# A weight-composing token kernel on one core: the first batch of the token stage gets an order of its own on VectorE and ScalarE, the two parts of B3 are made ahead of the last weight pass, and one low part of W1 is made a step sooner

## What is computed

```python
x = x + L0(x)   # x @ W0.T + (x @ A0[label0]) @ B0.T * 0.5
x = x + L1(x)   # x @ w_eff.T,  w_eff = quantised(W1 + delta) * scale + delta,  delta = B1 @ A1 * 0.5
x = x + L2(x)   # x @ W2.T + (x @ A2[label2]) @ B2.T * 0.5
x = x + L3(x)   # x @ W3.T + 2 * sum_e gate[e] * (x @ A3[e].T) @ B3[e].T
# gate: softmax over the best two of the 8 logits x @ Wr.T (+5 on the label's expert)
```

## Time and profile before

| | |
|---|---|
| median of 3 runs | 611.8 us (611.38 to 611.91) |
| the profiled execution | 611.85 us, its span 609.9 us |
| TensorE busy | 599.9 us, 98% of the span |
| VectorE / ScalarE / GpSimd busy | 392.5 (64%) / 214.0 (35%) / 80.4 us (13%) |
| granted clock of TensorE | full in all 40 slices |
| chain that ended last | PE 85%, DVE 10%, ACT 2%, DMA 2%, issue 1% |

### The profile page before, as it was taken

How to read it: one execution, slowest core, us unless ns; L and a number is a source line. 1 busy time by engine, 2 the same in 40 slices (tenths; PEclk the granted TensorE clock), 3 DMA queues, 4 the chain that set the end, 5 groups by cost and what they waited for, 6 DMA issues and landing times.

```text
span 609.9 us, 9220 instructions
## 1 busy us (share of the span) xinstructions
PE 599.9 (98%) x3247; PEld 536.0 (88%) x3247; DVE 392.5 (64%) x726; ACT 214.0 (35%) x402; POOL 80.4 (13%) x111
## 2 busy tenths in 40 slices
PE   7999999999999999999999999899999999999998
PEld 7999999899999999888888687688888888888887
DVE  3589998999998829100005688957474747475653
ACT  4444133346233138211111378433333333333331
POOL 2101010023000000000000015040404040403120
PEclk9999999999999999999999999999999999999999
DMA  9963220361000030200001200121221213130201
GB/s 266 261 170 99 82 70 1 43 218 68 1 1 1 1 35 7 38 1 0 0 0 34 69 2 2 52 87 54 85 75 63 82 56 98 39 118 19 96 8 70
DMA packets 57823, 37.68 MB, mean 62 GB/s; under 512 B 26684, under 2 KB 51516, under 8 KB 57796
## 3 DMA queue, kind: packets, MB, share of 16 engines
q1 hardware_dynamic: 57796, 37.31, 21.8%
HBM read 28.91 MB, written 8.39 MB: 61 GB/s over the span
## 4 chain that ended last, share of the span: by engine, by line
PE 85%; DVE 10%; ACT 2%; DMA 2%; issue 1%; SPq 0%; POOL 0%; DVEq 0%
PE acc L1356 46%; PE acc L1493 27%; PE acc L1514 4%; DVE q L1010 2%; PE acc L1516 2%; PE aux L1343 2%; DVE hg_lo L1036 1%; PE acc L1522 1%; DVE qtmp L1009 1%; PE acc L1523 1%; PE aux L1431 1%; DMA a_t<-in_L_cond_Wr_dram 1%; PE acc L1343 1%; DVE w_lo L914 1%; DMA w_raw<-in_L_cond_lora_B_w_dram 1%
## 5 line engine op out<-in xcount | busy, mean ns | idle before, releaser
L1356 PE MATMUL acc<-hg_hi,w_hi 128*128 128x352 f32 (+2 forms) x384 | 87.2, 335 | 0.4 <-DVE hg_lo L921 0.4
L1356 PE MATMUL acc<-hg_lo,w_hi 128*128 128x352 f32 (+2 forms) x384 | 85.8, 331 | 0.0
L1356 PE MATMUL acc<-hg_hi,w_lo 128*128 128x352 f32 (+2 forms) x384 | 85.7, 331 | 0.0
L1356 PEld LDWEIGHTS acc<-hg_hi,w_hi 128*128 128x128 f32 x384 | 66.3, 188 | 1.7 <-DVE hg_lo L921 0.6
L1356 PEld LDWEIGHTS acc<-hg_hi,w_lo 128*128 128x128 f32 x384 | 67.3, 188 | 0.0
L1356 PEld LDWEIGHTS acc<-hg_lo,w_hi 128*128 128x128 f32 x384 | 67.3, 188 | 0.0
L914 DVE TENSOR_TENSOR w_lo<-a_t,w_hi 128x1024 fp32r<-128x1024 f32 (+2 forms) x9 | 9.9, 1106 | 82.1 <-ACT w_hi L596 82.1
L1010 DVE TENSOR_TENSOR q<-q,qtmp 128x1024 f32<-128x1024 f32 x48 | 60.0, 1250 | 1.7
L761 ACT CAST left_hi<-xr 128x512 fp32r<-128x512 f32 x64 | 39.7, 622 | 54.4 <-PE acc L1493 34.7
L1493 PE MATMUL acc<-rh_a,left_hi 128*128 128x512 f32 (+1 forms) x132 | 52.7, 399 | 0.0
L532 POOL TENSOR_TENSOR xr<-xr 128x512 f32<-128x512 f32 x28 | 35.5, 1287 | 130.5 <-DVE left_lo L1159 129.2
(11 more groups left out here) (213 smaller groups left out, 1041.8 us busy)
## 6 DMA issues: line engine op xcount, KB each, us to landing
x_st<-in_x_dram SPq DMA_DIRECT2D x64, 128.0 KB, 2.8
out_dram<-part SPq DMA_DIRECT2D x31, 256.0 KB, 2.8
g<-in_L_cond_W_dram SPq DMA_DIRECT2D x8, 512.0 KB, 7.3
w_st<-in_L_cond_W_dram SPq DMA_DIRECT2D x8, 512.0 KB, 4.7
a_t<-in_L_cond_weight_dram SPq DMA_DIRECT2D x8, 512.0 KB, 5.0
w_raw<-in_L_cond_weight_dram SPq DMA_DIRECT2D x8, 512.0 KB, 4.0
a_raw<-in_L_cond_lora_A_dram SPq DMA_DIRECT2D x5, 128.0 KB, 3.6
a_raw<-in_L_cond_lora_A_dram SPq DMA_DIRECT2D x20, 32.0 KB, 2.0
```

What stands on the lines that cost most here:

```text
L1356: last = pe.matmul(acc[0:a.shape[-1], slot, bank * BANK:bank * BANK + c1 - c0], a[:, k, :], b[:, k, c0:c1], start=(at == 0 and n == 0), st ...
```

## The change

It has three parts.

1. In the second weight stage VectorE makes `w1_low(3)` ahead of `quantise(5, 2)` instead of behind it.
2. B3's high part (now two tiles of 512 columns at other places, `b3_hi0` and `b3_hi1`) and its low part are made just ahead of the last weight pass, where they were made in batch 0. The small tiles `hg`, `gate`, `top_i` and `hl1` change places with them.
3. Batch 0 of the token stage has its own written order on ScalarE and VectorE. The sum `S3` is split after `S2` and `S1` (tuple `LEFT_FIRST`, function `left_count`), and TensorE gets a wait for `S3` ahead of `M7`. The order of TensorE's products, GpSimd's list and SyncE's list stay as they are, and so does every other batch on ScalarE and VectorE.

```diff
+    LEFT_FIRST = ("A12", "A11", "A21", "A22", "S2", "S1", "S3", "S4")
...
-        b3_hi = place("b3_hi", 32768, [P, D], F32R)
+        b3_hi = [place("b3_hi0", 203776, [P, HD], F32R), place("b3_hi1", 126720, [P, HD], F32R)]
...
             evacuate(bp[0:R, :], 0, R, R, C_ALL)
+            act.wait_ge(b3_copied, 1)
+            for half in range(2):
+                act.copy(b3_hi[half][:], b3_f[:, half * HD:(half + 1) * HD]).then_inc(b3_hd, 1)
...
             add_delta(6)
+            w1_low(3)
             quantise(5, 2)
-            w1_low(3)
...
             add_bp(slice(0, R), 0, slice(0, R), C_ALL)
+            for half in range(2):
+                dve.wait_ge(b3_hd, half + 1)
+                cols = slice(half * HD, (half + 1) * HD)
+                dve.tensor_tensor(b3_lo[:, cols], b3_f[:, cols], b3_hi[half][:].bitcast(F32),
+                                  ALU.subtract).then_inc(b3_done, 1)
...
                 if first:
-                    pe.wait_ge(b3_done, 1)
+                    pe.wait_ge(b3_done, 2)
                 finish("Y", 0, 0)
 
+                wait_left("S3")
                 pe.wait_ge(part_copied, count(b, COPIES, "M6"))
```

VectorE's new list of batch 0 (ScalarE's follows the same pattern):

```diff
+                if first:
+
+                    v_copy(0)
+                    right_low("B21", 3)
+                    v_low(0)
+                    v_copy(1)
+                    right_low("T4", 3)
+                    m_low(0)
+                    v_low(1)
+                    left_low(b, "S2")
+                    right_low("T2", 3)
+                    best_two(0)
+                    m_low(1)
+                    gated(0)
+                    left_low(b, "S1")
+                    right_low("T1", 3)
+                    best_two(1)
+                    gated(1)
+                    g_low(0)
+                    left_low(b, "S3")
+                    for k in range(HALF):
+                        third_low(k)
+                    left_low(b, "S4")
+                    right_low("B22", 0)
+                    g_low(1)
+                    dve.wait_ge(l_split, LEFT.index("S4") + 1)
+                    x_turn(b, 0, 1)
+                    for k in range(1, HALF):
+                        right_low("B22", k)
+                    out("C11", "Y", "F11", "M1")
+                    left_low(b, "A12", 1)
+                    left_low(b, "A11", 1)
+                    out("C21", "W", "F21", "M7")
+                    out("C22", "X", "F22", "M5")
+                    sel_low(b + (E_FIRST + 1))
+                    x_turn(b, 1, 1)
+                    left_low(b, "A21", 1)
+                    left_low(b, "A22", 1)
+                    out("C12", "Z", "F12", "M6")
+                    return
```

More of the change, by code:

```diff
@@ L97, in count, with left_count @@
         return b * len(names) + (ahead * len(names) + names.index(name) + 1)
+    def left_count(b, name, ahead=0):
+        if isinstance(b, int) and b == 0 and not ahead:
+            return LEFT_FIRST.index(name) + 1
+        return count(b, LEFT, name, ahead)
     RIGHT = (("B11", 0), ("B21", 0), ("T4", 0), ("B11", 1), ("B21", 1), ("T4", 1), ("B11", 2), ("B21", 2), ("T4", 2),
@@ L857, in exponential @@
                     act.activation(gate[:, 24:25], gate[:, 25:26], ACT.Exp).then_inc(e_ready, 1)
-                if not first:
-                    copy_part("M1", "X")
+                if first:
+                    copy_second(0)
+                    right_high("T4", 3)
+                    v_high(0)
+                    copy_second(1)
+                    left_high(b, "S2")
+                    m_high(0)
+                    v_high(1)
+                    right_high("T2", 3)
+                    copy_part("M1", "X")
+                    done("M2")
+                    left_high(b, "S1")
+                    m_high(1)
+                    right_high("T1", 3)
+                    exponential(0)
+                    left_high(b, "S3")
+                    for k in range(HALF):
+                        third_high(k)
+                    done("M4")
+                    left_high(b, "S4")
+                    exponential(1)
+                    g_high(0)
+                    copy_part("M6", "X")
+                    for k in range(HALF):
+                        right_high("B22", k)
+                    act.wait_ge(sel_ready, SEL_FIRST + 2)
+                    sel_high()
+                    copy_part("M5", "Z")
+                    g_high(1)
+                    copy_part("M7", "X")
+                    left_high(b, "A12", 1)
+                    left_high(b, "A11", 1)
+                    left_high(b, "A21", 1)
+                    done("M3")
+                    left_high(b, "A22", 1)
+                    return
+                copy_part("M1", "X")
                 copy_second(0)
                 left_high(b, "S3")
-                if first:
-                    right_high("T4", 3)
                 v_high(0)
-                if first:
-                    right_high("T2", 3)
                 copy_second(1)
@@ L1157, in left_low @@
             def left_low(b, name, ahead=0):
-                dve.wait_ge(l_hd, count(b, LEFT, name, ahead))
+                dve.wait_ge(l_hd, left_count(b, name, ahead))
                 dve.tensor_tensor(left_lo[:, SLOT[name]], RAW[name], left_hi[:, SLOT[name]].bitcast(F32),
@@ L1320, in pair @@
                     left_low(b, "A21", 1)
[L1321 to L1325, removed]
-                out("C22", "X", "F22", "M5")
[L1327 to L1334, removed]
+                    out("C22", "X", "F22", "M5")
+                    left_low(b, "A22", 1)
+                    out("C12", "Z", "F12", "M6")
+                    return
+                dve.wait_ge(part_copied, count(b, COPIES, "M5"))
+                c12 = parts[PART_OF["C12"]][:]
+                add_or_take(c12, c12, parts[PART_OF["M5"]][:], ALU.add, last_sum)
+                out("C22", "X", "F22", "M5")
+                dve.wait_ge(last_sum, 1)
+                out("C12", "Y", "M3", "M6", HALVES[0])
+                out("C12", "W", "F12", "M6", HALVES[1])
             base = link.n
@@ L1523, in finish @@
                     pe.matmul(at, vm[h][:], vb_lo[:, cols], start=False, stop=False, skip_group_check=True)
-                    three(at, (hgt_h[h][:], hgt_l[h][:]), (b3_hi[:, cols], b3_lo[:, cols]),
+                    three(at, (hgt_h[h][:], hgt_l[h][:]), (b3_hi[half][:, c], b3_lo[:, cols]),
                           stop=True).then_inc(step_done, 1)
```

50 lines of the change are left out of this document (13 added, 37 removed).

## The result

The changed kernel took 608.05 us, the median of 5 runs (607.4 to 609.49); the kernel before took 611.86 on the same chip, also 5 runs (611.38 to 612.13). The ratio is 0.9941, 95% interval 0.9926 to 0.9955: 3.8 us faster, against a forecast of 608.3. The profiled execution took 607.86 us.

What follows compares the result with a forecast made beforehand. TensorE, busy 98% of the span, was taken as the bound, so only its pauses could yield gain. Batch 0 -3.9, batch 1's head +0.2, part 1 +0.25: -3.45 from 611.8 gives 608.3 us, range 607.3 to 609.4.

Steps and rivals of the forecast that it cites:

- Part 1: Second weight stage: the pause at delta(7) goes, but VectorE idles 1.6 us and pass 14 starts later; +0.25 us, a loss.
- Part 2: Ahead of the last weight pass: 1.9 us of VectorE's idle time cover 1.2 us of work; cost 0.
- Part 3: Batch 0 of the token stage: of 4.61 us lost, 0.4 stays at turn_v(0) and 0.3 at W; -3.9 us.
- a sign of being wrong: Batch 0: VectorE's second gate, forecast to end at 383.1, ending after 383.5 would show the prediction wrong.
- Head of batch 1: Start of batch 1: GpSimd's later sums hold VectorE's low part of S3; +0.2 us, bounds 0 and +1.3.
- Rival 1: Second weight stage: pass 14 isn't held by VectorE, 0.5 us gained instead of 0.25 lost; 607.6 us, chance 0.08.
- Rival 2: Batch 0: VectorE becomes the bound, an early 0.5 us delay is paid once, plus batch 1's hold; 609.95 us, chance 0.14.
- Rival 3: Batch 1: the hold takes all four GpSimd sums, 2.8 us lost instead of 0.2; 610.95 us, chance 0.04.
- Rival 4: After batch 0: VectorE's lag costs 0.6 us at mix(0) in each of 7 batches; 612.35 us, chance 0.03.

Runs made afterwards that it cites:

- B3 alone: Kernel before with only the two parts of B3 made ahead of the last weight pass, batch 0 in its old order: 610.14 us, ratio 0.9983.
- the tail alone: Kernel before with the new order only behind batch 0's second gate, on ScalarE and VectorE; B3 as before: 609.65 us, ratio 0.9973.
- B3 late: Changed kernel with B3's parts made in batch 0 again, just ahead of g_low(0): 608.86 us, ratio 0.996 to the kernel before.
- part 1 alone: Kernel before with only w1_low(3) moved ahead of quantise(5, 2): 611.81 us, ratio 1.0003.
- the third experiment: Kernel before with, in batch 0, g_high(1) ahead of ScalarE's cast of A12 and g_low(1) ahead of VectorE's transposes: 613.53 us, ratio 1.0028.
- more sums on GpSimd: Changed kernel with two spare 128 x 512 operations on GpSimd behind batch 0's sum for T3: 608.8 us, ratio 0.9944 to the kernel before.

## Why the prediction was right, and where its reading was not

**Part 1** (+0.25 predicted, +0.25 measured as a mean). The chain of steps holds: 1.60 us idle ahead of `w1_low(3)` (1.6 predicted), pass 12 free, the gain lost at pass 14. In all fourteen traces the token stage starts 164.01 to 164.05 us after `w1_low(5)`, so what the change does to this stage is to shift the start of that low part. The size can't be read from one pair of traces. Five have the old order, and their stages are 197.02 to 197.31 us long, with 0.15 to 0.42 us of pause at `delta(7)`; seven have the new order, and theirs are 197.37 to 197.42. The means differ by 0.25 us, single pairs by 0.06 (the pair in the result) to 0.40. The new pause was forecast with 0.7 to 0.9 us: the weight load shows 0.82, the matmul's bracket 0.53.

**Part 2** (0 predicted). The two low parts took 1.27 us from 352.38, and VectorE's timeline still has idle time ahead of the last operation of the stage:

```profile
352.38 1.27 DVE L1229 TENSOR_TENSOR b_lo<-b_f,b_hi 128x512 fp32r<-128x512 f32 x2
...
363.11 1.15 DVE L1171 TENSOR_TENSOR e_all<-ce,e_all 128x952 fp32r<-128x952 f32 x1 [0.86 <-ACT e_all L780]
```

Their room in batch 0 is worth 1.00 us in the old order and 1.20 in the new.

**Part 3** (-3.9 predicted, -3.74 measured). The walk through VectorE's new list held to 0.4 us: `v_copy(1)` at 372.23 (372.1), `g_low(0)` behind the second gate at 383.50 (383.1), `C22` amid the row that ends at 394.18, in time for batch 1 with no bracket. The gate thus ended on the edge of the 383.5 us that the prediction had named as a sign of being wrong. TensorE paid for it at the weight loads of Y (0.25, none predicted) and W (0.43, predicted 0.3).

**Where the reading failed.** "For what stood ahead of the late operation" gave each pause a cause of its own, and W's was the cast that waits for the transposed tokens. Each pause did go when its late operation came sooner, but its size was not gained: the cast's wait taken away, 1.30 us gone at W came back as 1.80 at `C22`; `v_copy(1)` ahead, 1.02 gone became 0.42 at Y and 0.33 at the narrow product. VectorE's own busy time says the same. In this stretch of the kernel before (370 to 398 us) it is

```profile
370.00:398.00 28.00, 24.32 (x113) 19.06 (x111) 26.25 (x65) 15.69 (x34) 4.13 (x9) 1.00 0.12 37
```

busy for 26.25 of 28 us while TensorE is for 24.32, and its longest wait is 0.25 us, for the load of tokens ahead of the second transposes. In the new order it waits once, for 0.27, between `v_copy(1)` and `C22`, and 0.6 us of work ahead of the gate costs 0.54. So the pauses were one backlog of VectorE, paid by `C22` at the latest; in the old order the load adds to it on the way to `C22`. The two runs with a single operation moved decide this; B3 alone and the tail alone fit both theories at the pauses that they remove. The sum came out right because it rested on a walk through the whole list, up to `C22`, and not on those causes. The gain is where work left that stretch: 1.66 us for the tail (work put behind `C22`), 1.00 for B3's parts, and 3.74 - 1.66 - 1.00 = 1.08 for the head, a remainder that no run measured alone (with B3 late, 2.54 - 1.66 = 0.88 remain). The head moves the low parts of `S3` and `S4` behind the gate and `v_copy(1)` ahead, and shortens the hold; how these three share it stays open.

TensorE's new wait for `S3` cost nothing: batches 2 to 6 take 29.76 to 29.80 us each in both kernels.

**Head of batch 1** (+0.2 predicted, -0.08 measured). The hold is there: `S3`'s low part began amid GpSimd's sums, which ended at 401.40, and took 1.11 us. It ended 0.55 us behind them, and `mix(0)` had the time to spare. The prediction had 0.5 us of spare time and a hold of up to 0.8; the hold was 0.4 to 0.5. Part 3 gained 0.16 us less than its term and the head lost 0.28 us less, so the two errors partly cancel in the sum.

**The rivals.** Rival 1 is refuted by part 1 alone. Rival 2's mechanism is real and its trigger did not come: VectorE is the bound of batch 0 already, and an early delay is paid once, as the rival has it (0.54 for 0.6 of work, 0.88 for two GpSimd operations). Rival 3 would need VectorE held through all four of batch 1's sums; it was held for the rest of one. Rival 4 falls with batch 1's 29.88 us and with VectorE's 2.09 us of idle time ahead of 400.13, which take up the lag. The bound at which it decides is 3.65 / 7 = 0.52 us a batch, not 0.53.

## What to carry to other kernels

Several pauses of one engine that wait for the same other engine, with no idle time on that one between them, are one backlog: read them as a sum, walk the busy engine's whole list up to the last thing that is waited for, and move work past that point or out of the stretch. Taking away the cause of a single pause moves it, and it can come back longer: look for a load that starts only when an operation of that list has read its buffer, since moving this operation back moves all that waits for the load. An operation moved ahead pays with the idle time in front of it: fill that with something from behind.

## What the runs showed of the hardware

In the trace of the third experiment a pause of 1.80 us of TensorE, behind smaller ones, was followed by a stretch at the 1.2 GHz level, 1.6 us of loss; the kernel before has pauses up to 1.30 us in this stage and its granted clock stays full. That the pause is the cause is not shown: two of the seven executions kept the full clock, and one of the changed kernel's five, 609.49 us, has a mean of 0.997 too, while the matmuls of its profiled execution show no pause over 0.53 us from 160 us on.

The hold by GpSimd is regular. In four cases (before: 1.68 us; changed kernel: 0.89 and 1.11; more sums on GpSimd: 1.53) a subtraction with two SBUF inputs that began amid a GpSimd operation on SBUF ended 0.55 us after it, which is near the 0.6 us of its own work. A copy on GpSimd holds as well: in the kernel before, `T4`'s low part took 0.88 us from 373.14, where GpSimd copied from 372.92 to 373.47, again 0.55 us behind. `v_copy(1)`, with one PSUM and one SBUF input, ran 0.29 us at 372.23, amid the sum of 371.49 to 372.78. GpSimd was held in turn: its sum at 401.58 took 1.52 us instead of 1.29 beside VectorE's held low part, which ended at 401.95. The Trainium skill, "SBUF — State Buffer", section "SBUF: two separate sides", says that whichever of the two starts first keeps the shared ports for its whole instruction while the other waits; the cases above agree, in both directions.
